# Attention and routed experts on one Trainium2 core: who adds beta, how the O^T scratch is laid out, who splits the half tiles' weights, and what TensorE does before the first data

## What is computed

```
x = L0_attn_X                                   # 8 x 512 x 256
xn = _layernorm(x)
# attention, 16 heads of 64, per sequence:
A1, A2 = Q1 @ K1^T / 8, Q2 @ K2^T / 8           # two score maps per head
P = softmax(A1) - lam * softmax(A2)
Y = concat_heads(P @ V) @ Wo + bo
attn = (layernorm(Y) * gamma + beta) * 0.2
# feed-forward, 8 experts, each token to its best one:
h = gelu(xn @ w1[e] + b1[e]);  y = h @ w2[e] + b2[e]      # 256 -> 1024 -> 256
ffn = y * route_prob_max
out = x + attn + ffn
```

## Time and profile before

| | |
|---|---|
| runs of the kernel before, median (lowest to highest) | 1843.43 us (1838.34 to 1845.68), 3 runs |
| the profiled execution: its own time | 1841.33 us |
| its span, first to last instruction | 1839.5 us |
| busy, TensorE matmul / VectorE / ScalarE / GpSimd | 97% / 84% / 77% / 36% |
| attention stage | 0 to about 1469 us |
| expert tiles 0 to 22 | about 1469 to 1726 us |
| output stage | about 1726 us to the end |
| mean granted TensorE clock | 0.992 |

### The profile page before, as it was taken

One profiled execution on the slowest core, in us unless ns is written; L12 is line 12 of the kernel. 1 busy time (PEld: TensorE's weight loads), 2 busy tenths in 40 slices (PEclk: granted clock), 3 DMA queues, 4 the chain that ended last, 5 costly groups with the idle time before them and its releaser, 6 DMA issues. The chain is left out here.

```text
span 1839.5 us, 32514 instructions
## 1 busy us (share of the span) xinstructions
PE 1789.6 (97%) x10474; PEld 1392.6 (76%) x10474; DVE 1538.1 (84%) x2636; ACT 1409.6 (77%) x3358; POOL 663.9 (36%) x717
## 2 busy tenths in 40 slices
PE   5999999999999999999999999999999999999997
PEld 4777777777777777777777777777677699999997
DVE  3988898899889888988898889888999866887467
ACT  4898888888888888888888888888788776676422
POOL 2444222222222222223222222222237455556554
PEclk8999999999999999999999999999999999999899
DMA  7899988888888888888888888888877586667698
GB/s 232 228 247 251 247 226 220 224 236 219 218 226 237 224 222 228 233 223 218 235 232 214 212 234 225 220 218 231 227 206 185 177 311 230 241 234 269 199 361 282
DMA packets 212915, 427.77 MB, mean 233 GB/s; under 512 B 28080, under 2 KB 107952, under 8 KB 206736
## 3 DMA queue, kind: packets, MB, share of 16 engines
q1 hardware_dynamic: 207744, 411.20, 80.1%
q0 software_dynamic: 4688, 13.51, 2.2%
q10 hardware_dynamic: 320, 1.05, 0.2%
HBM read 175.17 MB, written 49.15 MB: 122 GB/s over the span
## 5 line engine op out<-in xcount | busy, mean ns | idle before, releaser
L609 ACT ACTIVATE e<-p_score,nmax 128x512 f32<-128x512 f32 x1024 | 697.1, 688 | 134.1 <-DVE nmax L956 132.7
L475 POOL TENSOR_SCALAR e<-e,rrec,lam 128x512 f32<-128x512 f32 x512 | 394.0, 770 | 981.5 <-DVE rrec L923 981.0
L956 DVE TENSOR_REDUCE nmax<-p_score 128x2 f32<-128x1024 f32 x512 | 622.8, 1216 | 149.9 <-PE p_score L1101 145.8
L1101 PE MATMUL p_score<-ks,qs 128*128 128x512 f32 x2048 | 581.2, 406 | 13.8 <-ACT e L609 9.4
L1101 PEld LDWEIGHTS p_score<-ks,qs 128*128 128x128 f32 x2048 | 366.4, 189 | 184.6 <-issue 62.2
L1064 PE MATMUL p_proj<-xh,w 128*128 128x512 f32 x1024 | 386.2, 418 | 4.5 <-DVE xl L682 1.6
L930 DVE SCALAR_TENSOR_TENSOR pm<-e,rrec 128x512 f32<-128x512 f32 x512 | 382.8, 748 | 0.4 <-POOL e L475 0.2
L561 ACT COPY pT<-p_tr 128x512 f32<-128x512 f32 x512 | 301.7, 589 | 101.6 <-PE p_tr L1113 101.3
L1113 PE MATMUL p_tr<-consts,pm 128*128 128x128 f32 x2048 | 308.5, 273 | 1.7 <-ACT pT L561 1.6
L1113 PEld LDWEIGHTS p_tr<-consts,pm 128*128 128x128 f32 x2048 | 249.2, 140 | 80.2 <-issue 20.1
L1130 PE MATMUL p_pv<-pT,v 128*64 128x512 f32 x1024 | 247.7, 605 | 0.7 <-ACT pT L561 0.7
(11 more groups left out here) (211 smaller groups left out, 1832.9 us busy)
## 6 DMA issues: line engine op xcount, KB each, us to landing
ks<-k_parts SPq DMA_DIRECT2D x508, 256.0 KB, 4.8
qs<-q_parts SPq DMA_DIRECT2D x512, 128.0 KB, 4.3
w<-weight_parts_scratch SPq DMA_DIRECT2D x56, 1024.0 KB, 10.5
w<-in_w SPq DMA_DIRECT2D x46, 1024.0 KB, 7.1
oT_parts_scratch<-oT SPq DMA_DIRECT2D x32, 512.0 KB, 6.1
op<-oT_parts_scratch SPq DMA_DIRECT2D x32, 512.0 KB, 8.9
wv<-weight_parts_scratch SPq DMA_DIRECT2D x56, 256.0 KB, 5.5
weight_parts_scratch<-w SPq DMA_DIRECT2D x8, 1024.0 KB, 5.8
```

What stands on the lines that cost most here:

```text
L475: nc.gpsimd.tensor_scalar(e2, e2, rrec[:, g % 4, 1:2], lam[:, 0:1], ALU.mult, ALU.mult).then_inc(s_e2, 1)
L609: nc.scalar.activation(ex[:, g % EX, m, :], p_score[g % 2][:, m, :], ACT.Exp, bias=nmax[:, g % 2, m:m + 1], accum_out=rsum[:, g % 4, m:m + ...
L956: vec.tensor_reduce(nmax[:, g % 2, :], p_score[g % 2][:, :, :], AXX, ALU.max, negate=True).then_inc(s_max, 1)
L1101: last_op = nc.tensor.matmul(p_score[g % 2][:, m, :], qs[j][u][:, m, qt * P:(qt + 1) * P], ks[j][u][:, m, part, :], start=(part == 0), sto ...
```

## The change

1. In the prologue TensorE makes 12 transposes of the identity when the constants are there, and 8 more before the first projection. Their results are never read.
2. The spread of pair 0's first k is issued by ScalarE and SP, two transfers each. SP loads pair 2's raw V weights right after it and a wait for `high_v(0)`, with `load_raw(2)`, ahead of pair 0's other spreads, and `load_raw_v(3)` ahead of the x loads. ScalarE calls `high_v(2)` in step 3, not step 0; `high_v(0)` and `high_v(1)` stand earlier.
3. Both O^T scratches, and the tiles `oT` and `op`, are laid out by partition and group: a group's load reads 4 KB (whole) or 8 KB (parts) in one run per partition, where it read 1 KB runs. The parts come in one transfer. A store of a whole pair writes two runs of 1 KB per partition where it wrote one of 2 KB.
4. In half tiles, w2's low part is made by VectorE in the next tile (GpSimd keeps the last tile's half), w1's first high part is made at the start of the tile by VectorE, and its second by ScalarE after the high part of g 2.
5. Output weights are prepared from tile 7, and the loop ends two tiles sooner.
6. After tile 22: `load_parts(1)` goes ahead of `load_parts(2)`, then the store of expert rows, then `load_whole(2)`; `add_b2` of tile 22 goes right after `low_o(0)`.
7. Beta is added to x by VectorE in `base`; `add_beta` on GpSimd is gone.
8. TensorE takes a group's parts first (pair 7 down to 4) and waits for the split of the whole ones only before pair 3.

```diff
+WARM = (12, 8)
             spread(0, "q", 0)
+            sp.wait_ge(s_lo, 2)
+            spread_by(sp, 0, "k", 0, (1,))
+            sp.wait_ge(s_wvhi, 1)
+            load_raw_v(2)
+            load_raw(2)
             for what in "qk":
                 spread(1, what, 0)
+            sp.wait_ge(s_wvhi, 2)
+            load_raw_v(3)
             for n in range(PER_BATCH, 2 * PER_BATCH):
                 load_x(n)
-            load_raw(2)
-            for pair in (2, 3):
-                load_raw_v(pair)
...
-                if g == 1:
+                if g == 4:
                     low_v(2)
...
             high_qk(0, 1)
+            high_v(0)
             high_part(0, "q0")
             high_part(0, "k0")
             act.wait_ge(s_lo, 2)
-            spread_by(act, 0, "k", 0)
-            high_v(0)
+            spread_by(act, 0, "k", 0, (0,))
...
             high_part(0, "k1")
+            high_v(1)
             scale_q(1)
             high_qk(1, 0)
             high_qk(1, 1)
-            high_v(1)
...
-                if g == 0:
+                if g == 3:
                     high_v(2)
...
             pe.wait_ge(s_const, 16)
+            keep_warm(WARM[0])
             for n in range(PER_BATCH):
                 transpose_x(n)
+            keep_warm(WARM[1])
             for what in ORDER:
                 project(0, what)
...
-                    sp.dma_start(oW_d[h, :, a:b], oT_whole).then_inc(s_ost, 16)
+                    sp.dma_start(oW_d[:, a:b, h, :], oT_whole).then_inc(s_ost, 16)
...
-        WO_FROM = 9
+        WO_FROM = 7
...
-        LOOP_END = PAIR_TILES // 2 - 4
+        LOOP_END = PAIR_TILES // 2 - 5
...
-                sp.dma_start(of[n % 2][:, :, :], oW_v[:, :, n * G:(n + 1) * G]).then_inc(s_of[n % 2], 16)
+                sp.dma_start(of[n % 2][:, :, :], oW_d[:, n, :, :]).then_inc(s_of[n % 2], 16)
...
-                for c in range(2):
-                    sp.dma_start(op[n % OPS][:, c, WHOLE:PAIRS, :].bitcast(F32), oP_v[:, c, :, n * G:(n + 1) * G]
-                                 ).then_inc(s_op[n % OPS], 16)
+                sp.dma_start(op[n % OPS][:, WHOLE:PAIRS, :, :].bitcast(F32), oP_d[:, n, :, :, :]
+                             ).then_inc(s_op[n % OPS], 16)
...
             turns(body, before_last=first_o)(sp)
+            load_parts(1)
             load_parts(2)
-            load_parts(1)
+            store(FFN_TILES - 1, 0, 1)
             load_whole(2)
-            store(FFN_TILES - 1, 0, 1)
...
-                if n == 0:
+                if n == 0 or PAIR_TILES <= n < FFN_TILES - 1:
                     continue
...
-            pool.wait_ge(s_scaled, 1)
-            pool.wait_ge(s_w2lo_dve, 1)
-            for n in range(R):
-                add_beta(n)
...
             for n in range(GROUPS):
                 fetch(n)
-                if n >= R:
-                    add_beta(n)
...
+                    if g == X_AT + 1 and t.half_follows():
+                        act.wait_ge(s_w1[1 - j], 16 * (t.half_next + 1))
+                        act.wait_ge(s_h, HG * n)
+                        nc.scalar.copy(w1p[1 - j][:, 0, 1, :], w1[1 - j][:, 1, :]).then_inc(s_w1hi_act, 1)
...
+            def w2_low(n):
+                dve.wait_ge(s_w2hi, n + 1)
+                v.tensor_tensor(w2p[n % 2][:, 1, :, :], w2[n % 2][:, :, :], w2p[n % 2][:, 0, :, :].bitcast(F32),
+                                ALU.subtract).then_inc(s_w2lo_half, 1)
...
+                early = t.half_follows()
+                if early:
+                    w1_high(n + 1, 1 - j, t.half_next, 0, False)
+                if t.exact and t.fs_before == 1 and t.fs == 1:
+                    w2_low(n - 1)
                 for g in range(HG):
...
             turns(body, after=output_weights)(dve)
-            for n in range(OPS):
+            low_o(0)
+            add_b2(FFN_TILES - 1, 0, LOOPED // 2, False, 1)
+            for n in range(1, OPS):
                 low_o(n)
-            add_b2(FFN_TILES - 1, 0, LOOPED // 2, False, 1)
 
             def base(n):
 
                 r = n % R
+                dve.wait_ge(s_x[r], 16 * (n // R + 1))
+                v.tensor_tensor(x[r][:, :, :], x[r][:, :, :], beta.unsqueeze(1).to_broadcast([P, 2, E]), ALU.add
+                                ).then_inc(s_xb, 1)
...
-                    for k in range(PAIRS):
+                    for k in range(PAIRS - 1, -1, -1):
+                        if s == 0 and k == PAIRS - 1:
+                            pe.wait_ge(s_op[c], 16 * (n // OPS + 1))
+                        if s == 0 and k == WHOLE - 1:
+                            pe.wait_ge(s_olo, n + 1)
...
-    oW_d = nc.dram_tensor("oT_whole_scratch", [WHOLE, P, T], F32).ap()
-    oP_d = nc.dram_tensor("oT_parts_scratch", [PAIRS - WHOLE, P, 2, T], F32).ap()
+    oW_d = nc.dram_tensor("oT_whole_scratch", [P, GROUPS, WHOLE, GROUP], F32).ap()
+    oP_d = nc.dram_tensor("oT_parts_scratch", [P, GROUPS, PAIRS - WHOLE, 2, GROUP], F32).ap()
```

More of the change, by code:

```diff
@@ L294, in front_stage, with spread_by @@
         HALF = KT * 2 * P
-        def spread_by(queue, u, what, pair):
+        def spread_by(queue, u, what, pair, maps=range(2)):
             j = pair % 2
             src = parts[what][u]
-            for m in range(2):
+            for m in maps:
                 a = src[m * D:(m + 1) * D]
@@ L567, in copy_o @@
                 if whole(pair):
-                    nc.scalar.copy(oT_whole, p_pv[:, :]).then_inc(s_o, 1)
+                    nc.scalar.copy(oT_whole, p_pv[:, :].rearrange("p (g s) -> p g s", s=GROUP)).then_inc(s_o, 1)
                 else:
-                    nc.scalar.copy(oT[:, 0, :], p_pv[:, :]).then_inc(s_ohi, 1)
+                    nc.scalar.copy(oT[:, :, 0, :], p_pv[:, :].rearrange("p (g s) -> p g s", s=GROUP)).then_inc(s_ohi, 1)
             root()
@@ L1028, in group_pair, with keep_warm @@
                 return PAIRS * (n // PER_BATCH - 1) + X_PAIRS[n % PER_BATCH]
+            def keep_warm(count):
+                for _ in range(count):
+                    nc.tensor.transpose(p_tr[:, 0, :], ident, ident)
             def ranks():
@@ L1323, in ffn_and_output_stage, with w2_low_done @@
         LOOPED = FFN_TILES - 1
-        LOOP_END = PAIR_TILES // 2 - 4
+        LOOP_END = PAIR_TILES // 2 - 5
         assert LOOPED % 2 == 0 and PAIR_TILES % 2 == 0
+        def w2_low_done(engine, n):
+            if isinstance(n, int) and n >= PAIR_TILES:
+                engine.wait_ge(s_w2lo_half, n - PAIR_TILES + 1)
+            else:
+                engine.wait_ge(s_w2lo, n + 1)
         def op_free(engine, n):
@@ L1331, in op_free @@
             elif n == 1:
-                engine.wait_ge(s_w2lo, FFN_TILES)
+                engine.wait_ge(s_w2lo_half, HALF_TILES - 1)
+                engine.wait_ge(s_w2lo, PAIR_TILES + 1)
                 engine.wait_ge(s_w2lo_dve, 1)
@@ L1358, in x_in_middle, with half_follows @@
                 return self.exact and self.has(1) and (self.n == 0 or self.fs_next == 1)
+            def half_follows(self):
+                return self.exact and self.fs == 1 and self.has(1)
             def second(self):
@@ L1407, in body @@
                     sp.wait_ge(ahead.s_last_lo, 1)
-                    sp.dma_start(oP_d[PAIRS - 1 - WHOLE, :, :, T - S:T], ahead.oT[:, :, :].bitcast(F32)).then_inc(s_oT, 16)
+                    sp.dma_start(oP_d[:, GROUPS - PER_BATCH:GROUPS, PAIRS - 1 - WHOLE, :, :],
+                                 ahead.oT[:, :, :, :].bitcast(F32)).then_inc(s_oT, 16)
                     first_of_output()
@@ L1499, in _ @@
                                         ALU.subtract).then_inc(s_w2lo, 1)
-            def add_beta(n):
-                pool.wait_ge(s_x[n % R], 16 * (n // R + 1))
-                nc.gpsimd.tensor_tensor(x[n % R][:, :, :], x[n % R][:, :, :],
-                                        beta.unsqueeze(1).to_broadcast([P, 2, E]), ALU.add).then_inc(s_xb, 1)
             def fetch(n):
@@ L1566, in body @@
                     act.wait_ge(s_oT, 16 * (B * PAIRS - 1))
-                    nc.scalar.copy(ahead.oT[:, 0, :], ahead.p_last[:, :]).then_inc(ahead.s_last_hi, 1)
+                    nc.scalar.copy(ahead.oT[:, :, 0, :], ahead.p_last[:, :].rearrange("p (g s) -> p g s", s=G)
+                                   ).then_inc(ahead.s_last_hi, 1)
             def output_weights(n):
@@ L1582, in high_o @@
                 op_free(act, n)
-                nc.scalar.copy(op[n % OPS][:, 0, 0:WHOLE, :], of[n % 2][:, :, :]).then_inc(s_ohi, 1)
+                nc.scalar.copy(op[n % OPS][:, 0:WHOLE, 0, :], of[n % 2][:, :, :]).then_inc(s_ohi, 1)
             turns(body, after=output_weights)(act)
@@ L1662, in body @@
                     if t.has(1) and not t.first() and not t.second():
-                        if g < KT:
+                        if g < KT and not early:
                             w1_high(n + 1, 1 - j, t.half_next, g, not t.after(1))
-                        else:
+                        if g >= KT:
```

(12 more changed lines are left out.)

36 lines of the change are left out of this document (18 added, 18 removed).

## The result

The changed kernel takes **1819.71 us** (median of 4 runs, 1818.95 to 1821.46), the kernel before 1842.76 us on the same chip (4 runs, 1838.34 to 1845.68). The ratio is 0.9878, 95% interval 0.9857 to 0.9900: 23 us faster. The profiled execution took 1818.95 us, its span is 1817.1 us (before: 1841.33 and 1839.5), and the mean granted clock 0.996 (0.992).

A forecast was written before the change was run, and what follows sets the result against it. TensorE is busy nearly throughout, so gains lie in the prologue, half tiles and output stage: 11.0 + 1.8 + 4.7 + 7.0 + 1.0 = 25.5 us off 1841.3, plus 2.1 for the median, gives 1818 us, range 1808 to 1830.

The forecast's parts named there:

- the likeliest case: Whole kernel: faster, chance 0.94, against 0.03 for the same and 0.03 for slower.
- Prologue: Start of the attention stage: early transposes 2.0, pair 2's V weights 7.5 and clock after the stall 1.5, together 11.0 us.
- V weights' stall: Prologue: ScalarE's wait for pair 2's V weights goes; 7.6 us reckoned, 7.5 taken.
- is covered by about 8 us: Prologue: spreads and x loads moved behind 0.75 MB on SP are delayed some 2 us, with about 8 us to spare.
- Rival 3: Prologue: transfers are then what steps 3 to 8 wait for, half of the 11 remains, 1823 us; chance 0.06.
- Early transposes: Prologue: pair 0's first twelve projection matmuls run 0.23 us apart in place of 0.43, gaining 2.0 us.
- Clock after the stall: Prologue: TensorE has no such idle time before step 3; 1.5 us of VectorE's 1.89 goes, bounds 0 and 3.3.
- Half tiles and tile 22: Last expert tiles: shorter waits in half tiles gain 1.8 us; no low clock in tile 22 gains 4.7.
- Rival 2: Last half tiles: the clock falls all the same, since waits of 0.5 remain, 1823 us; chance 0.13.
- Output stage: Output groups: faster transfers and no gap before group 1 remove 7.0 of 9.1 us of gaps, bounds 2 and 9.1.
- rival 5: Output stage: new scratch reads run at half rate, 185 GB/s, making the kernel slower, 1891 us; chance 0.03.
- Tail: After the last output matmul: VectorE is no longer late beside GpSimd's adds, net 1.0 us, bounds 0 and 2.

The follow-up runs named there:

- a2: Changed kernel with the old prologue whole (no early transposes, old first-k spread, pair 2's V weights loaded late and called for in step 0): 1823.91 us.
- a3: Changed kernel with the split of pair 2's first weights moved to step 4 of pair 0 (ScalarE from step 2, GpSimd from 3): 1818.93 us.
- c1: Kernel of a3, with the next sequence's x loads and the store of pair 1's weights issued after pair 1's first spreads: 1819.97 us.
- d2: Changed kernel with both the swap of b5 and the later weight split of a3: 1814.69 us, ratio 0.9855 to the kernel before.
- a1: Changed kernel without the 12 and 8 early transposes of the identity: 1821.81 us, ratio 0.9890 to the kernel before.
- d0: Changed kernel itself, unaltered, run again as reference on the chip of the d runs: 1820.35 us, ratio 0.9885 to the kernel before.
- a4: Changed kernel with O^T scratches and tiles laid out as before (1 KB runs, parts in two transfers), load order kept: 1825.87 us.
- b4: Changed kernel with the old half tiles (w2's low part by GpSimd in the same tile, w1's high parts both by VectorE): 1823.52 us.
- b1: Changed kernel with beta added by GpSimd again, ahead of the fetches and between them: 1817.71 us, ratio 0.9884 to the kernel before.
- b5: Changed kernel with VectorE making w1's second low part before the low part of h of g 3 in half tiles that a half tile follows: 1817.30 us.
- d3: Kernel of b5 run again, beside the unaltered changed kernel on the same chip: 1817.12 us, ratio 0.9868 to the kernel before.
- d1: Changed kernel without the stores of the parts of pairs 0 and 1 (2.5 MB), part of attention computed from other weights: 1816.83 us.

## Why the prediction was right

The time was forecast at 1818.0 and came out at 1819.7, inside the range, faster as the likeliest case said. That it was missed by only 1.7 is in part luck. The sum gave 25.5 us and 22.4 were gained, and of these 3.1 us 1.3 came back because the median of the changed kernel stands 0.8 above its profiled run, where 2.1 were added. Within the sum two large terms were off, in opposite directions.

1. **Prologue, 11.0 forecast, 5.9 measured (5 to 6 by a2).** This is what failed. The V weights' stall went as reckoned: step 3 came 7.4 us sooner. The failed step is the sentence that SP's delay "is covered by about 8 us" and the list of what is late next, scores and maxima "in turn". It followed the loads and spreads past which the V weights were moved, but not the stores behind them, on which ScalarE waits before it reuses a weight tile. That wait was in the code before and hidden in the stall; uncovered it costs ScalarE 3.79 us, and 3.24 to 5.30 in the other profiles with this prologue. The lead of 9.2 us at step 4 is 6.8 at step 5. Another 1.0 goes between steps 5 and 16, and no run shows by what. To take the store's wait away is not enough: in a3, c1 and d2 the next transfer is awaited in its place. Rival 3, half of the 11 remains, had the size right and steps 3 to 8 as the place; it had been given 0.06.
2. *Early transposes, 2.0 forecast:* projections run at 0.23 us a matmul, as said, but scores of step 0 wait for the spread of k and start 0.7 us sooner than before, and those of step 1 only 0.3. A faster step ahead of a transfer only lengthens the wait for it; a1 suggests that the low clock behind the longer wait takes the rest, in its one profile.
3. *Clock after the stall, 1.5 forecast:* it came at first, since from step 3 to 4 it takes 3.15 us in place of 4.93, and is lost with the rest of the lead behind the new wait. The low clock there is not what loses it: in d0, a4 and b4 the clock does not fall behind that wait, and step 16 starts at 71.75 to 71.99 all the same.
4. *Half tiles and tile 22, 1.8 + 4.7 forecast, 1.5 + 4.7 measured;* the waits were put at 0.5 and are 0.45, the tiles at 9.0 apart and are 9.11, with w1's second low part last on VectorE. Rival 2 did not come.
5. *Output stage, 7.0 forecast, 8.9 measured.* TensorE now binds. The estimate of 2.94 us a half group holds to the hundredth. The layout gave 4.9; the other 4.0 is put down to the order, which no run undoes alone. The term was too small because the gaps were taken to stay in part. The Trainium skill, "DMA: Bandwidth & Descriptors", section Bandwidth, has the HBM side bind at about 358 GB/s, but the same section gives that figure as a core's share when both cores of a pair stream, and has measured 425 GB/s for one core alone. The 398 GB/s over 60 us and the 412 of the first loads agree with the latter; no run here has a second core at work.
6. *Slower, the scratch at half rate (rival 5):* 412 GB/s at a share of 0.99 in the first loads; no loss is seen at partition pitches of 64 and 128 KB. The Trainium skill's lower rates (same page, section Latency and other measured facts) begin at 512 KiB; no run here has such a pitch.
7. *Tail, 1.0 forecast, 1.4 measured,* but not for beta: b1, with beta on GpSimd, has 7.8. Two profiles of one kernel differ by 1.0 (8.6 and 9.6, against one profile of 10.0 before), so it is not shown that the tail gained at all.

## What to carry to other kernels

When a long wait is taken away, list every wait that its engine passes in the stretch after it, the ones for stores that free a tile among them: each was hidden, and the largest is the new one. When an engine's last piece of work in a tile gates the next tile, look whether something that is needed later stands in front of it; here a swap of two VectorE instructions gave 3.3 us. Where profiles differ in a stage that was not edited, as the prologue does here by 3 us, compare stages and not whole spans. Before a low clock is blamed for a loss, look for a profile of the same kernel without it.

## What the runs showed of the hardware

- A full DMA share can mean half the rate: 214 GB/s at 1.02 in 22 to 24 us, when the spread of k is under way beside a load of raw weights, and 412 at 1.10 in 38 to 40 us, among the stores of weights. No run isolated the spreads:

```profile
22.00:24.00 2.00, 0.00 (x0) 0.00 (x0) 0.00 (x0) 1.98 (x3) 1.68 (x2) 1.00 1.02 214
...
38.00:40.00 2.00, 0.15 (x2) 0.00 (x0) 0.00 (x0) 1.22 (x3) 0.00 (x0) 1.00 1.10 412
```

- The same O^T in runs of 4 and 8 KB instead of 1 KB and with one transfer for a group's parts instead of two takes less of the engines' time, 398 GB/s at 1.03 against 364 at 1.09 (a4).
- Before step 0 the clock fell behind waits of TensorE of 3.69 us (a2), 3.97 (before) and 4.75 or more (every profile with the transposes), and not behind one of 3.39 (a1). Before the projections ahead of step 5 it fell behind 2.67 us or more (changed, b1, b5, d3, a1), and not behind 2.36 or less (a4, b4, d0, d1). In the half tiles it fell where waits were 0.85 to 1.17 us a tile, in two profiles in two different tiles, and in no profile where they were 0.45.
- A VectorE subtraction of 128x256 with two operands in SBUF takes 0.43 us alone. Begun while GpSimd splits w2, it ends 0.27 to 0.37 us after GpSimd's subtraction in all thirteen cases that the traces of the kernel before and of b4 show by themselves in half tiles, whether it then shows 0.42 or 2.10 us. What it loses is the rest of GpSimd's instruction. VectorE's 128x256 addition of b2, whose first operand lies in PSUM, takes 0.41 us beside the same GpSimd instruction.
